# Adaptive-LayerNorm block of retention and Hadamard FFN on one core: loop over batches against eight unrolled units

## What is computed

```python
# x: (4, 512, 256); everything is float32
mod = (silu(c) @ wmod).reshape(4, 6, 1, 256)            # sa, ca, ga, sb, cb, gb
ga, gb = sign(g) * max(abs(g), 0.25)                    # for g in ga, gb
h = layernorm(x) * (1 + ca) + sa
x = x + ga * retention(h)      # q, k with rope, v, gate: 4 heads, dk 32, dv 64, decay per head
                               # o = causal(q k^T) v + q S; rms norm over dv * gnorm * silu(gate); @ Wo.T
h = layernorm(x) * (1 + cb) + sb
x = x + gb * ffn(h)            # fwht(silu(h W1^T) * (h W3^T)) W2^T, 1024 hidden columns, fwht = Hadamard/32
```

## Time and profile before

| | us |
|---|---|
| median of 3 runs | 310.13 (309.5 to 311.9) |
| span of the profiled execution, first to last instruction | 311.4 |
| PE busy, PEld busy | 266.3, 229.4 |
| DVE busy, POOL busy, ACT busy | 213.0, 172.1, 116.4 |

### The profile page before, as it was taken

The page is one execution under the profiler, slowest core; times in us unless marked ns, Lnnn a source line. Parts: engine busy times, 40 slices in busy tenths (PEclk is TensorE's granted clock), DMA queues, the critical chain, the costliest instruction groups (busy, mean ns, idle before and its releaser), DMA issues.

```text
span 311.4 us, 4414 instructions
## 1 busy us (share of the span) xinstructions
PE 266.3 (86%) x1488; PEld 229.4 (74%) x1488; DVE 213.0 (68%) x431; ACT 116.4 (37%) x231; POOL 172.1 (55%) x188
## 2 busy tenths in 40 slices
PE   0699849945299999996999999969999999699993
PEld 0678438834178989986789889867898998588882
DVE  3769997589967487698864876999648778921112
ACT  1312743541123564332235643322366433232230
POOL 1349976597425736564357465554573656461333
PEclk9997955558579999997999999999999999999999
DMA  6991400000000000000200000001000000020001
GB/s 201 426 389 45 135 0 0 0 2 0 2 1 0 2 0 0 2 0 0 67 0 0 0 0 0 0 0 67 0 0 0 0 0 0 2 68 0 2 0 67
DMA packets 6563, 11.52 MB, mean 37 GB/s; under 512 B 660, under 2 KB 4756, under 8 KB 6424
## 3 DMA queue, kind: packets, MB, share of 16 engines
q1 hardware_dynamic: 6552, 11.38, 10.2%
...
## 4 chain that ended last, share of the span: by engine, by line
PE 62%; DVE 21%; issue 6%; POOL 5%; ACT 2%; DMA 2%; POOLq 1%; SPq 0%; DVEq 0%; ACTq 0%
PE pu L305 21%; PE pacc L305 12%; PE pc L305 9%; PE pa L305 5%; PE pb L305 4%; DVE xn L671 4%; POOL rso L882 2%; DVE stats L657 2%; DMA wmod_sb<-wmod 2%; DVE qk L654 2%; POOL rs L888 1%; PE pa L411 1%; PE pstate L305 1%; DVE hid L695 1%; DVE xn L638 1%
## 5 line engine op out<-in xcount | busy, mean ns | idle before, releaser
L893 POOL TENSOR_TENSOR hid_lo<-hid,hid_hi 128x512 fp32r<-128x512 f32 x31 | 41.3, 1334 | 50.6 <-ACT hid_hi L811 50.6
L305 PE MATMUL pu<-h_hi,w_hi 128*128 128x512 f32 x128 | 52.2, 408 | 2.5 <-DVE h_lo L686 2.5
L305 PE MATMUL pu<-h_lo,w_hi 128*128 128x512 f32 x128 | 51.5, 402 | 0.0
L305 PE MATMUL pu<-h_hi,w_lo 128*128 128x512 f32 x128 | 51.2, 400 | 0.0
L695 DVE TENSOR_TENSOR hid<-silu,pu 128x512 f32<-128x512 f32 x32 | 21.8, 682 | 34.1 <-PE pu L305 26.7
L305 PE MATMUL pacc<-w_hi,hid_hi 128*128 128x256 f32 x128 | 37.8, 295 | 0.1
L305 PE MATMUL pacc<-w_lo,hid_hi 128*128 128x256 f32 x128 | 36.5, 286 | 0.0
L305 PE MATMUL pacc<-w_hi,hid_lo 128*128 128x256 f32 x128 | 36.5, 285 | 0.0
L811 ACT ACTIVATE hid_hi<-hid 128x512 fp32r<-128x512 f32 x32 | 20.1, 627 | 32.4 <-DVE hid L695 17.1
L305 PEld LDWEIGHTS pu<-h_hi,w_hi 128*128 128x128 f32 x128 | 24.6, 192 | 8.2 <-DVE h_lo L686 2.9
L806 ACT ACTIVATE silu<-pu 128x512 f32<-128x512 f32 x32 | 19.1, 595 | 27.0 <-PE pu L305 26.9
...
## 6 DMA issues: line engine op xcount, KB each, us to landing
...
out<-xres SPq DMA_DIRECT2D x8, 256.0 KB, 2.1
...
xres<-x SPq DMA_DIRECT2D x2, 256.0 KB, 3.1
...
```

The lines of the kernel that those rows point to most:

```text
L305: mm = pe.matmul(ps, a, c, start=start and n == 0, stop=stop and n == len(ops) - 1, skip_group_check=True)
L893: pool.tensor_tensor(hid_lo[:, k % 2], hid32[:, k % 2], hid_hi[:, k % 2].bitcast(F32), ALU.subtract).then_inc(p_hid.sem, 1)
```

## The change

The loop is gone: all work is written out, in eight units of 256 tokens (two tiles, half a batch; unit u is half u % 2 of batch u // 2). `WINDOW` is one stretch of the order, and there are eight of them. Window w holds the FFN of unit w (`f`), the late part of the attention of unit w+1 (`l`: scores to second LayerNorm), the early part of unit w+2 (`e`: modulation, projections, transposes), the statistics of unit w+3 (`n`), and the rest of the FFN of unit w-1 (`p`). Parts:

- FFN per unit: `up.k` makes two hidden chunks of 256 tokens side by side in one bank, so its matmuls are 256 wide instead of 512, and there are twice as many over the whole kernel (768 for 384). `down.k` takes two chunks; there is one bank `pacc`.
- Hadamard fold on TensorE: the butterflies go; for each of eight output chunks, 16 matmuls of 256 columns with the 128x128 Hadamard matrix or its negative add up the eight split chunks of W2 (128 matmuls for 8).
- Block queries by DMA: the eight copies on ACT and DVE go; SP issues eight DMAs of 32 partitions per unit, four from `qkt_hi`, four from `qkt_lo`.
- Modulation of both LayerNorms moves from DVE to ACT (`Identity` with scale and bias).
- `gnorm` is folded into Wo, so that the product with the gate weights on POOL goes; ACT writes silu of the gate straight to `gg`.
- Rope's addition on POOL is one instruction per unit; the residual of the attention is added in place by DVE, so that L889 goes.
- The inverse root of the rms norm is made per tile (4 columns) instead of per two tiles (8).
- Weights have their own raw tiles, so that no load waits.

```diff
+WINDOW = ("l:sc.0 l:st.0 p:down.3 l:plo.0 l:sc.1 l:st.1 p:out e:ht e:h l:plo.1 e:hlo f:up.0 l:o.0 f:hid.0 l:ss.0 l:o.1 "
+          "l:ss.1 e:qk e:rope l:y.0 l:y.1 f:up.1 f:hid.1 l:yt l:ytlo e:vg.0 e:vlo.0 l:proj f:down.0 f:up.2 l:norm2 "
+          "f:hid.2 e:vg.1 e:vlo.1 n:stats l:h2t l:h2 e:kspl e:qkt e:qklo e:qb l:h2lo f:up.3 f:hid.3 n:norm f:down.1 "
+          "f:down.2")
+
+ORDER = FIRST + [s for w in range(UNITS) for s in steps(WINDOW, p=w - 1, f=w, l=w + 1, e=w + 2, n=w + 3)]
+FIRST = steps(
+    "0:stats 0:norm cols.0 zero wqk 0:ht 0:h wvg 0:hlo 1:stats 1:norm 0:qk 0:rope 0:vg.0 0:vlo.0 0:kspl 0:vg.1 hadr "
+    "0:qkt 0:vlo.1 0:qklo 0:qb cols.1 rows 1:ht 1:h 1:hlo w2r.0 w2r.1 0:sc.0 0:st.0 0:plo.0 0:sc.1 0:st.1 0:plo.1 "
+    "gates had.0 had.1 1:qk w2.0 0:o.0 0:ss.0 1:rope 0:o.1 0:ss.1 w13.0 1:vg.0 wo 0:y.0 1:kspl 1:vlo.0 0:y.1 had.2 "
+    "had.3 0:yt 0:ytlo w2.1 1:vg.1 2:stats 0:proj had.4 had.5 1:vlo.1 w2.2 1:qkt w13.1 0:norm2 1:qklo 1:qb 0:h2t 0:h2 "
+    "had.6 had.7 0:h2lo 2:norm w13.2 w2.3")
...
# SP
+                if kind == "qb":
...
+                    for of, dst, src in ((a_qkt, qb_hi, qkt_hi), (d_qklo, qb_lo, qkt_lo)):
+                        sp.wait_ge(of.sem, of.after(u))
+                        for h in range(HEADS):
+                            rows = slice(h * DK, (h + 1) * DK)
+                            sp.dma_start(dst[rows, :, h, :].bitcast(F32), src[rows, par, 0].bitcast(F32).rearrange(
+                                "p (t i) -> p t i", t=2)).then_inc(s_qb.sem, 16)
...
# PE
+                elif kind == "had":
...
+                    for j in range(HB):
+                        sign = bin(k & j).count("1") % 2
+                        for part in (w2r_hi, w2r_lo):
+                            mm = pe.matmul(phad[k // 2][:, k % 2 * D:(k % 2 + 1) * D], had_r[:, sign], part[:, j],
...
+                elif kind == "sc":
+                    if k == 0:
+                        pe.wait_ge(s_qb.sem, s_qb.per * (u + 1))
...
+                elif kind == "yt":
+                    pe.wait_ge(d_y.sem, d_y.after(u, 1))
+                    transposed(pc, y0, t_yt)
...
+                        for n in range(2):
+                            of = slice(n * P, (n + 1) * P)
+                            mm = three(ps[:, n * UT:(n + 1) * UT],
+                                       [((w13_hi[:, k, w, kc, of], w13_lo[:, k, w, kc, of]),
+                                         (h2_hi[:, par, kc], h2_lo[:, par, kc])) for kc in range(KC)])
...
# ACT
+            def modulated(dst, ps, b, n, done):
+                for kc in range(KC):
+                    ins = act.activation(dst[:, kc], ps[:, kc * UT:(kc + 1) * UT], ACT.Identity,
+                                         bias=mod_cols[:, b, n, kc:kc + 1], scale=mod_cols[:, b, n + 1, kc:kc + 1])
...
# POOL
+            def inverse_root(var, ve, root, scale, eps, made, done, value):
+                pool.tensor_scalar(ve, var, scale, eps, ALU.mult, ALU.add).then_inc(made.sem, 1)
+                pool.wait_ge(made.sem, value)
+                pool.tensor_tensor(root, ve, mhalf[:, 0:root.shape[-1]], ALU.pow).then_inc(done.sem, 1)
...
+                    pool.tensor_tensor(y0[:, k], yo[:, k], gg[:, par, k], ALU.mult).then_inc(p_y0.sem, 1)
+                    pool.wait_ge(d_ss.sem, d_ss.after(u, k))
+                    inverse_root(ss[:, u, k], vo[:, u, k], rso[:, u, k], 1.0 / DV, EPS, p_vo, p_rso, p_vo.after(u, k))
```

More of the change, by code:

```diff
@@ L49, with steps, __init__, after @@
 AX = mybir.AxisListType
[L52 to L70, removed]
[6 rows of a table removed]
-STEADY = steps("norm.0 up.0 h1.0 hid.0 norm.1 h1lo.0 up.1 h1.1 qk.0 h1lo.1 up.2 qk.1 hid.1 vg.0 qk.2 vg.1 vg.2 qk.3 "
[4 rows of a table removed]
-LAST = steps("up.0 up.1 hid.0 hid.1 up.2 up.3 down.0 up.4 hid.2 hid.3 down.1 up.5 hid.4 down.2 down.3 up.6 down.4 "
-             "hid.5 hid.6 up.7 down.5 hid.7 down.6 down.7 out.0 out.1")
-class Signal:
-    def __init__(self, sem, per, start=0):
-        self.sem, self.per, self.start = sem, per, start
-    def after(self, batch, k):
-        return batch * self.per + (self.start + k)
-def adaln_block_kernel(nc, x, c_t, w_qkvg, w_o, gnorm, w13, w2, wmod, consts, select, cos, sin, out):
+C_CAUSAL, C_HADAMARD, C_BLOCKS, C_END = 0, P, 2 * P, 2 * P + HEADS * DV
+def steps(text, **units):
+    out = []
+    for word in text.split():
+        unit, _, rest = word.rpartition(":")
+        kind, _, k = rest.partition(".")
+        u = units[unit] if unit in units else int(unit or 0)
+        if 0 <= u < UNITS:
+            out.append((kind, u, int(k or 0)))
+    return out
+FIRST = steps(
[5 rows of a table added]
+WINDOW = ("l:sc.0 l:st.0 p:down.3 l:plo.0 l:sc.1 l:st.1 p:out e:ht e:h l:plo.1 e:hlo f:up.0 l:o.0 f:hid.0 l:ss.0 l:o.1 "
[3 more added lines that the diff above has]
+ORDER = FIRST + [s for w in range(UNITS) for s in steps(WINDOW, p=w - 1, f=w, l=w + 1, e=w + 2, n=w + 3)]
+ORDER += steps("7:down.3 7:out")
+at = ORDER.index(("up", 0, 3))
+ORDER.insert(at, ("w13", 0, 3))
+class Signal:
+    def __init__(self, sem, per):
+        self.sem, self.per = sem, per
+    def after(self, u, k=0):
+        return u * self.per + k + 1
+def adaln_block_kernel(nc, x, c_t, w_qkvg, w_o, gnorm, w13, w2, wmod, ident_in, consts, select, trig, out):
     with ExitStack() as ctx:
@@ L288, in store @@
-            def store(f):
-                for n in range(2):
-                    sp.wait_ge(p_out.sem, p_out.after(f, n + 1))
-                    sp.dma_start(out[f, 2 * n * P:(2 * n + 2) * P].rearrange("(t p) d -> p t d", p=P),
-                                 xres[:, f, 2 * n:2 * n + 2]).then_inc(stored.sem, 16)
-            with sp.Fori(1, B) as b:
-                store(b - 1)
-            store(B - 1)
-            sp.wait_ge(stored.sem, stored.after(B, 0))
+            sp.dma_start(ident[:], ident_in).then_inc(in_id.sem, 16)
@@ L299, in _ @@
+            run(sp, step)
+            sp.wait_ge(stored.sem, stored.after(UNITS - 1, 15))
         @block.tensor
@@ L307, in three @@
                 return mm
-            def columns(parts, at, done):
-                for part in parts:
-                    for h in range(KC):
-                        col = part * D + h * P
-                        for kc in range(KC):
-                            mm = pe.matmul(pu1[:, at:at + B], wmod_sb[:, kc, col:col + P], sc_sb[:, kc, :],
-                                           start=(kc == 0), stop=(kc == KC - 1))
-                        at += B
-                mm.then_inc(done.sem, 1)
@@ L645, in step @@
                 elif kind == "proj":
-                    dve.wait_ge(t_wo.sem, t_wo.after(b, k + 1))
-                    if first and k == 0:
+                    if par == 0:
                         dve.wait_ge(a_gates.sem, B)
-                    pair = slice(2 * k, 2 * k + 2)
-                    dve.tensor_tensor(branch[k][:], pw[k][:, :].rearrange("p (t d) -> p t d", t=2),
+                    dve.wait_ge(t_wo.sem, t_wo.after(u))
+                    dve.tensor_tensor(tmp[:], pd[:, :].rearrange("p (t d) -> p t d", t=2),
```

1111 lines of the change are left out of this document (499 added, 612 removed), and 10 rows, old and new, of tables (FIRST, STEADY).

## The result

The changed kernel takes 370.25 us (median of 4 runs, 368.4 to 371.2) against 311.01 us before (4 runs, 309.5 to 312.7): ratio 1.189, 95% interval 1.185 to 1.194. It is 59 us slower. I forecast 323 us with a range of 300 to 337: the side was right, the size was not.

The account below looks back on a forecast made before the run. TensorE was taken to bound the loop; 69.3 us to window 0, windows of 30.8, 161.0, 31.0 and 18.7, DMA waits 8.4 and tail 4.9 made 324.1, so 323 us was forecast, range 300 to 337.

Parts of the forecast that it names:

- 29.7 us a window: Full window: sum of TensorE's matmuls and transposes at full clock, 29.7 us; with 2.5 us of waits, 32.2.
- POOL's chain between the hid splits: Window, ahead of y: gate product 0.74, sum 0.20, pow 1.0, twice; 2.1 us a tile, ending at 15.05, without gaps.
- the landing of the DMAs: Block queries: each DMA lands 2.1 us after its issue, the last of eight at 34.3 in the window.
- the width of 256 costs little: Up matmuls 256 wide instead of 512, 0.12 us each: 2.7 us more over the kernel.
- at full clock: Windows: TensorE's matmuls priced at 0.12 us for 256 columns and 0.23 us for 512.
- Rival (d): Half-clock Hadamard matmuls in the first stage, and norm2 colliding with POOL in each window: 335 us, chance 0.13.
- DVE's product (0.42): Window, rms product ahead of yt: takes 0.42 us, ends at 15.5, so TensorE waits 1.65 us.
- An issue takes 0.43 us, 0.47 start to start: Block-query DMAs: the last of eight starts 3.3 us after the first; wait 1.4 us in windows 1 to 6, 8.4 us.
- first Hadamard matmul at 38.4: First stage: fold starts at 38.4 us, after first scores at 30.1, masks, splits, state, gates matmuls and four gate copies.
- norm2 was forecast at 64.7: First stage: norm2, waiting on DVE behind splits of W2 and w13, put at 64.7 us; stage ends at 69.3.
- The three signs: Signs of a wrong forecast: windows below 31.5 us, first stage ending before 60, eight DMAs landed within 3.5 us of ACT's copy.
- Rival (a): Windows: interleaving covers the chains, with POOL's part of the y chain 1.7 us shorter; 301.5 us, chance 0.19.

Follow-up runs that it names:

- e11: e10 with the block queries copied by ACT and DVE, as before the change, instead of by DMA; 304.1 us, ratio 0.976.
- e4: The changed kernel with idle matmuls ahead of two waits of TensorE in each window (16 before the block queries, 12 before the rms product); 360.1 us.
- the pauses: e10 with TensorE held ahead of the first scores of units 2 to 7 by 1, 2, 4 or 6 ACT copies; 308.7, 312.8, 327.6, 338.8 us.
- e9: The changed kernel with POOL's rope addition made to wait until DVE's second rms product of the window is done; 356.2 us, ratio 1.142.
- e7: The changed kernel with the windows in a new order, window 6 apart, and w13's last split behind window 0's projection; 314.9 us, ratio 1.013.
- e10: e7 with a new order of the first stage, w13's last split at its end, and window 6 reordered again; 301.1 us, ratio 0.969.

## Why the prediction was wrong in size

Right: that TensorE bounds the loop (its 29.7 us a window measure 30.2, small waits included) and that work dropped on DVE, POOL and ACT is worth nothing there (shown for the copies alone: with them back, e11's windows 1 to 5 still take 30.2 us); which waits take the place, and with whom; POOL's chain between the hid splits (7 instructions without a gap, pow 1.0 us); the landing of the DMAs (1.9 for 2.1); the first stage up to the first scores (qk 14.2 for 14.3, scores 30.2 for 30.1); that the width of 256 costs little (0.12 us a matmul, as in the earlier trace rows; no run undid it).

Wrong, by the steps as they were put:

1. The sum priced every matmul of the windows "at full clock". The rows of the loop before showed 0.98, and I took it as a property of a busy TensorE. With two waits of 2.5 to 3 us in each window it is 0.91; this is the step that failed. It cost some 15 us in windows 0 to 5 (17.7 against my price of a window's work) and some 4 behind. The trace of the kernel before held a sign of it that I did not look for: the half clock behind one of its three waits of 2.8 us, shown above; the 0.98 is this one stretch and one at the loop's start. e4 shows it from one side and the pauses from the other: a wait of 2.70 us costs 4.4 to 4.7 us. Rival (d), "cold TensorE", had looked for it in the first stage only. The Trainium skill ("TensorE: Matmul & The Clock Gate", section HAM oscillation — how this bites in real kernels) describes this pattern, bursts of matmuls between waits that each start at half clock, for waits of 3 to 5 us. I had read that page for the spacing of matmuls and not for this; the trace agrees in the pattern, and has it behind shorter waits, of 2.5 to 3 us, most but not all of the time.
2. "DVE's product (0.42)" ahead of yt: 1.48 beside POOL's addition. I had asked whether POOL collides with norm2, a DVE instruction with one tensor input, and not with the product, which has two; norm2 took 0.73 for both (as taken), and the second product met rope's addition in every window that has an early part. With it the wait is 2.46 to 2.96 for 1.65 (e9: 1.41 to 1.90 without).
3. "An issue takes 0.43 us, 0.47 start to start": for the 32-partition copies 0.60 and 0.64. Eight of them end 1.2 us later: 2.9 us a wait instead of 1.4.
4. The first stage, "first Hadamard matmul at 38.4", came at 42.35. The gates matmuls alone take 7.2 us, at half clock:

```profile
34.38 2.07 PE L298 MATMUL pacc<-tmp,h32b 4*128 4x512 f32 x2
36.25 3.62 PE L298 MATMUL pu<-tmp,h32b 4*128 4x512 f32 x4
39.66 1.91 PE L298 MATMUL pacc<-tmp,h32b 4*128 4x512 f32 x2
42.35 0.55 PE L310 MATMUL pacc<-w2r_hi,had_r 128*128 128x256 f32 x1 [0.78 <-ACT gates L632]
```

   I named them and gave them no price. norm2 was forecast at 64.7 and its transposes started at 71.8, 7.1 us late, 4 of which are these; what the other 3 are was not followed.
5. Missed: the last piece of `w13` is split in window 0, behind what DVE has there; TensorE waits 4.6 us and runs at half clock for 4 more (1.8 us). It was in the order, and I had not followed it.

The three signs by which I would have seen myself wrong (windows below 31.5 us, a first stage under 60, DMAs landed within 3.5 us) all lie on the faster side, and none of them came true, though the forecast was wrong by 47 us. A small slip changes nothing: by the formula that the prediction takes from the Trainium skill the narrower matmuls cost 1.0 us more, not 1.1.

Rival (a), that the interleaving covers the chains, was put at 301.5 us and 0.19. It is not what this order does; but e7 to e10 show that the units and parts of the change can do it, with POOL's roots ahead of hid.0 as (a) had supposed. The loss was of neither the units, the fold nor, past their place, the DMAs.
